# Order of the three product groups in the expert stage of a decoder layer

## The reference

```
gate_up = jnp.einsum('ecd,edm->ecm', buf, w_up_gate)      # 256 -> 2 * 176
gate, up = jnp.split(gate_up, [I], axis=-1)
h = jax.nn.silu(gate) * up
out_buf = jnp.einsum('eci,eid->ecd', h, w_down)           # 176 -> 256
```

## Time and profile before

| what | value |
|---|---|
| median of 3 runs | 798.91 us |
| profiled execution, its own time | 800.48 us |
| its span, first to last instruction | 798.5 us |
| TensorE busy in the span | 745.3 us (93%) |
| VectorE, ScalarE, GpSimd busy | 574.3, 467.6, 543.1 us |
| mean granted TensorE clock | 0.989 |
| expert stage, first up product to the first product of the shared MLP's second half | 644.35 to 729.18 us |

### The profile page before, as it was taken

One profiled execution on the slowest core, in us unless ns is written; L12 is line 12 of the kernel. 1 busy time (PEld: TensorE's weight loads), 2 busy tenths in 40 slices (PEclk: granted clock), 3 DMA queues, 4 the chain that ended last, 5 costly groups with the idle time before them and its releaser, 6 DMA issues.

```text
span 798.5 us, 14037 instructions
## 1 busy us (share of the span) xinstructions
PE 745.3 (93%) x4364; PEld 625.8 (78%) x4364; DVE 574.3 (72%) x1536; ACT 467.6 (59%) x1163; POOL 543.1 (68%) x459
## 2 busy tenths in 40 slices
PE   5799999999999999999999999998999989899992
PEld 4577788888888888887777888777778878898761
DVE  6967886768777767778887777898572357775685
ACT  5557776766676767666567666565623255653432
POOL 4457998787878887778888988778533534433663
PEclk9999999999999999999999999999999999999997
DMA  9411346422122222221222222221151134532332
GB/s 299 126 46 53 91 159 184 147 68 68 67 67 68 67 68 67 68 64 57 69 74 73 87 73 56 65 74 48 54 159 41 64 142 174 183 144 86 110 98 90
DMA packets 47748, 75.73 MB, mean 95 GB/s; under 512 B 9728, under 2 KB 24640, under 8 KB 47680
## 3 DMA queue, kind: packets, MB, share of 16 engines
q1 hardware_dynamic: 43504, 65.19, 25.9%
q0 software_dynamic: 3072, 8.39, 3.3%
q10 hardware_dynamic: 1104, 1.31, 0.5%
HBM read 57.71 MB, written 17.17 MB: 94 GB/s over the span
## 4 chain that ended last, share of the span: by engine, by line
PE 73%; DVE 11%; issue 7%; ACT 4%; POOL 2%; DMA 2%; DVEq 0%; ACTq 0%; POOLq 0%
PE ps L432 21%; PE ps L968 16%; PE ps L933 13%; PE ps L984 9%; PE ps L954 7%; PE ps L1130 5%; DVE q_sw L1312 1%; DVE q_sw L1311 1%; DVE hid_both L1643 1%; POOL slot_inputs L1784 1%; DVE hid_hi L1633 1%; POOL o_lo L1768 1%; DVE hid L1638 1%; DVE hid L1630 1%; DMA kvh_rows<-hc_t 1%
## 5 line engine op out<-in xcount | busy, mean ns | idle before, releaser
L968 PE MATMUL ps<-pt,vp 128*128 128x512 f32 (+3 forms) x512 | 149.5, 434 | 10.3 <-DVE q_sw L1312 10.1
L633 ACT ACTIVATE prob<-ps,neg_max 128x512 f32<-128x512 f32 (+3 forms) x256 | 132.5, 525 | 33.4 <-DVE neg_max L1321 30.6
L968 PEld LDWEIGHTS ps<-pt,vp 128*128 128x128 f32 x512 | 82.7, 190 | 59.9 <-issue 30.5
L1749 POOL TENSOR_TENSOR q_sw<-q_cos,q_sw 128x512 f32<-128x512 f32 x62 | 79.2, 1277 | 65.9 <-DVE q_cos L1313 65.8
L1321 DVE CUSTOM_DVE_ANT_0 ps<-ps,causal_row 128x512 f32<-128x512 f32 (+3 forms) x256 | 120.2, 511 | 4.6 <-PE ps L933 4.5
L642 ACT ACTIVATE pt<-ps,vcol 128x512 f32<-128x512 f32 x64 | 44.2, 690 | 109.4 <-PE ps L954 109.4
L1768 POOL TENSOR_TENSOR o_lo<-o_t,o_hi 128x512 fp32r<-128x512 f32 x64 | 84.4, 1318 | 33.4 <-ACT o_hi L671 33.4
L954 PE MATMUL ps<-id_f,prob 128*128 128x128 f32 x640 | 92.3, 275 | 0.9 <-ACT pt L642 0.9
L933 PE MATMUL ps<-k_hi,q_hi 128*128 128x512 f32 x248 | 86.6, 349 | 0.4 <-POOL q_lo L1753 0.3
L1340 DVE TENSOR_TENSOR o_t<-ps,inv_row 128x512 f32<-128x512 f32 x64 | 44.3, 692 | 52.5 <-PE ps L968 52.5
L1753 POOL TENSOR_TENSOR q_lo<-q_sw,q_hi 128x512 fp32r<-128x512 f32 x62 | 80.2, 1294 | 2.6 <-ACT q_hi L665 2.3
(11 more groups left out here) (218 smaller groups left out, 1942.3 us busy)
## 6 DMA issues: line engine op xcount, KB each, us to landing
kh_row<-kvh_rows SPq DMA_DIRECT2D x64, 256.0 KB, 3.2
inv_row<-inverse_sums SPq DMA_DIRECT2D x64, 256.0 KB, 3.1
slot_inputs<-zeros SPq DMA_DIRECT2D x8, 640.0 KB, 4.9
xg<-slot_inputs SPq DMA_DIRECT2D x8, 640.0 KB, 4.5
slot_outputs<-yo SPq DMA_DIRECT2D x8, 640.0 KB, 3.3
up_raw<-in_w_up_dram SPq DMA_DIRECT2D x8, 368.0 KB, 4.5
wo_raw<-in_wout_dram SPq DMA_DIRECT2D x4, 512.0 KB, 7.9
dn_sb<-in_w_dn_dram SPq DMA_DIRECT2D x8, 256.0 KB, 3.5
```

The costliest lines, as they stand in the source:

```text
L633: ins = act.activation(prob[:, i % 2, ROW_AT[nt]:ROW_AT[nt] + w], ps_s[bank][:, at:at + w], ACT.Exp, scale=-1.0, bias=neg_max[:, i % 2, nt ...
L968: ins = pe.matmul(ps_qo[:, mt * P:SEQ], vp[:, b * TPB + mt, :], pt[:, i % 2, cols], start=(mt == 0), stop=(mt == PT_BANKS[-1][-1]))
L1749: pool.tensor_tensor(q_sw[:], q_cos[:], q_sw[:], ALU.add).then_inc(q_sum_ready, 1)
```

## The change

TensorE makes the 48-row group (group 2) first, then groups 0 and 1. ScalarE takes the silu of the 48 rows first, then that of the 128 rows. VectorE does the three instructions of the 48 rows first, then those of the 128 rows. Counts on the semaphores follow. No instruction is added or removed.

```
 ScalarE, expert_steps
                         act.wait_ge(gu_psum, 3 * (2 * e + c) + 1)
+                        act.activation(sg2[0:H2, c, :], ps[5][0:H2, 0:HC], ACT.Silu).then_inc(silu_ready, 1)
+                        act.wait_ge(gu_psum, 3 * (2 * e + c) + 2)
                         act.activation(sg[:, c, :], ps[3][:, 0:HC], ACT.Silu).then_inc(silu_ready, 1)
-                        act.wait_ge(gu_psum, 3 * (2 * e + c) + 3)
-                        act.activation(sg2[0:H2, c, :], ps[5][0:H2, 0:HC], ACT.Silu).then_inc(silu_ready, 1)
 TensorE, expert_up
-                for k, (a, z) in enumerate(((0, P), (P, 2 * P), (2 * P, UPW))):
+                for k, a, z in ((2, 2 * P, UPW), (0, 0, P), (1, P, 2 * P)):
+                    if k == 2:
+                        pe.wait_ge(gu_free, 2 * m + 1)
                     if k == 0:
-                        pe.wait_ge(gu_free, 2 * m + 1)
-                    if k == 2:
                         pe.wait_ge(gu_free, 2 * m + 2)
 VectorE, expert_steps
                         dve.wait_ge(silu_ready, 2 * m + 1)
-                        dve.wait_ge(gu_psum, 3 * m + 2)
+                        dve.tensor_tensor(hid2[0:H2, c, :], sg2[0:H2, c, :], ps[5][64:64 + H2, 0:HC],
+                                          ALU.mult).then_inc(gu_free, 1)
+                        dve.wait_ge(gu_free, 2 * m + 3)
+                        dve.tensor_copy(hid2_both[0:H2, cs], hid2[0:H2, c, :]).then_inc(hid_hi_ready, 1)
+                        dve.wait_ge(hid_hi_ready, 2 * m + 1)
+                        dve.tensor_tensor(hid2_both[LO:LO + H2, cs], hid2[0:H2, c, :],
+                                          hid2_both[0:H2, cs].bitcast(F32), ALU.subtract).then_inc(hid_ready, 1)
+                        dve.wait_ge(silu_ready, 2 * m + 2)
+                        dve.wait_ge(gu_psum, 3 * m + 3)
                         dve.tensor_tensor(hid[:, c, :], sg[:, c, :], ps[4][:, 0:HC], ALU.mult).then_inc(gu_free, 1)
...
```

More of the change, by code:

```diff
@@ L1628, in expert_steps @@
                         dve.wait_ge(silu_ready, 2 * m + 1)
-                        dve.wait_ge(gu_psum, 3 * m + 2)
+                        dve.tensor_tensor(hid2[0:H2, c, :], sg2[0:H2, c, :], ps[5][64:64 + H2, 0:HC],
[7 more added lines that the diff above has]
+                        dve.wait_ge(gu_psum, 3 * m + 3)
                         dve.tensor_tensor(hid[:, c, :], sg[:, c, :], ps[4][:, 0:HC], ALU.mult).then_inc(gu_free, 1)
-                        dve.wait_ge(gu_free, 2 * m + 3)
+                        dve.wait_ge(gu_free, 2 * m + 4)
                         dve.tensor_copy(hid_hi[:, cs], hid[:, c, :]).then_inc(hid_hi_ready, 1)
-                        dve.wait_ge(hid_hi_ready, 2 * m + 1)
+                        dve.wait_ge(hid_hi_ready, 2 * m + 2)
                         dve.tensor_tensor(hid_lo[:, cs], hid[:, c, :], hid_hi[:, cs].bitcast(F32),
                                           ALU.subtract).then_inc(hid_ready, 1)
[L1637 to L1644, removed]
                     if not (last and r == 1):
```

## The result

The changed kernel takes 794.35 us (median of 6 runs, 792.77 to 796.23) against 800.1 us for the kernel before beside it: ratio 0.9931, 95% interval 0.9913 to 0.995. The forecast was no difference that can be told; the changed kernel is about 5.5 us faster by the ratio. The profiled execution took 794.02 us, its span is 792.0 us (before 800.48 and 798.5).

What follows compares the result with a forecast made beforehand. TensorE was taken to wait for VectorE's nearly full chain. 4 x 0.03 + 2 x 0.16 - 2 x 0.50 = -0.56, say -0.5 us, took 798.91 to 798.4 us; own range 797.4 to 799.8, chance 0.60.

Steps and rivals of the forecast that it cites:

- What bounds the kernel: Expert stage: TensorE's second down bank waits for the end of VectorE's twelve-instruction chain in all 8 experts, 7.7 us.
- The start: First half of an expert: VectorE's chain starts 0.57 after the silu, at 656.68 in place of 656.99, gaining 0.31 us.
- The meeting with GpSimd: SBUF port, first half: VectorE's rounding comes 0.08 us behind GpSimd's L1857, losing 0.94 us in all against 0.44 now.
- The pause: Second half: VectorE's wait for ScalarE's silu goes because down_head moves ahead; 0.17 us gained, in four experts only.
- Experts 6 and 7: No pause to gain there and a start about 0.37 earlier: -0.37 + 0.53 = +0.16 us each.
- Expert 5: Counted as a plain expert with experts 0, 1 and 3: +0.03 us.
- Experts 2 and 4: Table load delays the first silu; meetings with GpSimd cost 0.08 + 0.41 + 0.48 in place of 1.47: -0.50 us each.
- What TensorE waits for anew: Second half's group 0 waits for its banks: 0.17 us in plain experts, 0.4 in experts 2 and 4, covered by slack.
- B: VectorE gets to the port first: 0.5 us less in each of six experts, -3.5 in all, 795.4 us; chance 0.20.
- C: VectorE loses nothing to GpSimd, second-bank waits vanish, new bank waits stay: 5.7 us less, 793.2 us; chance 0.08.

Runs made afterwards that it cites:

- e2: Changed kernel with one more, always satisfied, VectorE wait between the 48-row silu wait and the 48-row multiplication; ratio 0.9967 to the kernel before.
- e4: Changed kernel with ScalarE's down_head held until the first half's third group has ended, as late as before the change; ratio 0.9956 to the kernel before.
- e3: Kernel before, VectorE's two waits ahead of the 128-row multiplication swapped (silu last) in every second half and first halves of experts 0, 2, 4; ratio 0.9989.
- e1: The changed kernel run and profiled again, nothing altered; ratio 0.9943 to the kernel before.

## Why the prediction was wrong

**What bounds the kernel: right.** TensorE waited for VectorE's chain: twelve instructions, 5.57 us in all, and what they lose. In the changed kernel expert 1's chain is 654.61 + 5.57 + 0.42 = 660.60, as in the trace.

**The start: mis-sized, and this is the step that failed.** I took 0.57 from silu to multiplication from a place where VectorE stands at two waits, in the loop, and put it at a place with one. There it is 0.46, and e2 shows that one wait more in the loop brings the 0.57 back. The gain at the start is 0.43 in place of 0.31 (T + 1.98 to T + 1.55, where T is the start of the expert's first product). By itself that is 0.12; it turned the next term, which was by far the larger miss.

**The meeting with GpSimd: the mechanism right, its outcome wrong.** L1857 does start 1.54 after the silu ahead of down_head (655.02 to 656.56), and L1858 follows it; in the twelve profiles they hold VectorE's instructions that work from SBUF to SBUF, while the multiplications take 0.49 in every case. But VectorE now comes 0.04 ahead and not 0.08 behind, so the meeting costs 0.42 and not 0.94. With the 0.11 put back (e2) nearly the 0.94 comes about: 0.51 and 0.42. For expert 1 the sum is then -0.43 - 0.17 + 0.42 - 0.44 = -0.62; the chain's end, counted from T, moved by -0.59 (8.13 to 7.54), and the expert is 0.60 shorter.

**The pause: right** where it could be seen (it is gone, and e4 brings it back).

**Experts 6 and 7:** +0.16 each was the same error; -0.50 and -0.60. **Expert 5** gained 0.5 more: L1850 met the chain's last instruction before (0.99) and now comes at 701.41, after that instruction (700.83, 0.49) has ended. The prediction goes through L1850 in experts 1 and 3 but not in expert 5; its +0.03 left this meeting as it was, without a reason. **Experts 2 and 4** were forecast at -0.50 and came to -0.55 and -0.65. Here the chain starts 0.11 earlier too, but the second silu follows the first after 0.34 (not the 0.44 of the prediction), so GpSimd comes 0.13 earlier and is still 0.53 ahead: the order at the port was never in doubt, and the rounding takes 0.38.

**What TensorE waits for anew: right.** In experts 2 and 4 the second half's second group starts 1.39 after its first (665.45 to 666.84), 0.51 more than a group takes, where 0.5 was forecast; elsewhere it is less than 0.1, where 0.17 was forecast. In experts 1, 3, 5 and 6 TensorE no longer stands idle at the second down bank, and they take 9.48 or 9.49 us.

**The rivals.** B, at 0.20, is what happened, for the reason it gave: "less than what I can vouch for". Its sum of -3.5 us against the 5.2 of the stage lacked the 0.11 at each start and expert 5. By size alone C, at 0.08, is nearest: its 5.7 us are what the runs show (5.5 by the ratio). That is a coincidence, since C had VectorE lose nothing to GpSimd and all waits at the second bank gone, while in the changed kernel the first half's rest takes 0.91 in all eight experts and four waits are left. My own text held the warning that every other offset of GpSimd costs less than the one I had found; a forecast that stands on the worst of all offsets, by 0.08 us, should have had a chance below 0.60.

## What to carry to other kernels

Where two engines hold each other up at a port, work out the order of arrival; if it hangs on less than 0.1 us, give both orders their price and an even chance. An offset taken from another place must come from the same number and kind of waits. Where one engine works without a pause and another waits for its end, ask first what it loses on the way: most of this change's gain (3.75 of 4.62 us in experts 1 to 7) is time no longer lost in meetings with GpSimd, and an earlier start by itself brought 0.87. In a loop, wait last for what comes last; it took 0.69 us off two experts in e3, and look at the meetings again afterwards, since the same edit made two others 0.17 longer.

## What the runs showed of the hardware

- One wait more in a loop, satisfied already, behind the one that ends last: 0.11 us (0.57 for 0.46); outside the loop nothing (0.46).
- Of two instructions that both work in SBUF, the one that starts first goes through and the other waits nearly to its end. VectorE's rounding came 0.04 ahead of GpSimd and took 0.33; 0.07 behind, and took 0.84. In the twelve profiles 111 of VectorE's SBUF-to-SBUF instructions in the expert stage are held by more than 0.2 us; all of them get on 0.14 or 0.15 us before the recorded end of GpSimd's instruction (recorded end of VectorE's, less its usual 0.33 or 0.49). A sharing of bandwidth would hardly give one fixed distance.
- The order is decided within 0.01 us: a rounding in the same hundredth as GpSimd's start was held (0.90, e3), one 0.01 ahead was not (0.33, kernel before). One such turn and what follows from it is 0.56 us of a 10 us expert.
- The granted clock fell in expert 0 in 6 of 12 profiles, of either order and not in others of the same kernel: the first 12 matmuls follow each other at 0.27 us in place of 0.147, and expert 0 takes 1.4 to 1.5 us more. TensorE had stood for 1.95 us ahead of it in all six, but also in three of the six without the fall. The stretch in e1, and the same in the first profile of the changed kernel (stretch, us; PE, PEld, DVE, ACT, POOL busy; granted clock; DMA share; GB/s):

```profile
644.00:648.00 4.00, 3.81 (x15) 3.82 (x16) 1.57 (x4) 0.94 (x3) 0.00 (x0) 0.57 0.61 239
648.00:652.00 4.00, 4.00 (x32) 3.99 (x31) 3.15 (x7) 2.34 (x7) 1.76 (x2) 1.00 0.00 0
```

```profile
644.00:648.00 4.00, 4.00 (x29) 3.92 (x29) 3.17 (x7) 2.54 (x7) 1.43 (x2) 1.00 0.36 147
```

A mean of 0.57 of full speed over 4 us is the lower level, 1.2 GHz, for most of this time and 2.4 GHz for the rest. What tells the executions apart is open.
- A table load of 1.28 us stands ahead of the first silu of each loop body; written out, experts 2 and 4 are 1.3 to 1.4 us shorter in the new order.
